# A reordered prologue with layer 0's input of the first sequence inside it, that sequence's buffers, and new places for the side pieces of the first and last turns

## What is computed

```python
# layer 0: two selective scans (one forward, one backward in time), 512 channels x 16 states
x_ssm = ln(x, norm1_g, norm1_b) * (1 + scale) + shift;  skip = x_ssm      # scale, shift, gate = silu(c) @ Wada.T + bada
x_ssm = ln(x_ssm, norm2_g, norm2_b)
mz = x_ssm @ Wz.T + bz;  act_mx = silu(x_ssm @ Wx.T + bx)
z1 = ssm(mz @ Wc1.T + bc1);  z2 = flip(ssm(flip(mz @ Wc2.T + bc2)))
x = x + gate * ((act_mx * z1 + act_mx * z2) @ Wf.T + bf + skip)
# layer 1: Mamba with a permutation of the tokens, a convolution of 4 taps and one selective scan
# layer 2: softmax attention, 16 heads;  layer 3: linear attention, 8 heads; both with a modulated norm and silu
# ssm(u): delta = softplus(..); h = exp(delta*A) * h + delta*B*u;  y = C . h, step by step over 256 tokens
```

## Time and profile before

| what | us |
|---|---|
| median of three runs | 3379.65 (3375.57 to 3383.61) |
| the profiled execution | 3382.8 |
| its span, first to last instruction | 3381.1 |
| TensorE, ScalarE, VectorE, GpSimd busy | 3058.3, 2878.3, 2690.2, 2666.1 |
| mean granted TensorE clock | 0.967 |

### The profile page before, as it was taken

The page is one execution under the profiler, slowest core; times in us unless marked ns, Lnnn a source line. Parts: engine busy times, 40 slices in busy tenths (PEclk is TensorE's granted clock), DMA queues, the critical chain, the costliest instruction groups (busy, mean ns, idle before and its releaser), DMA issues.

```text
span 3381.1 us, 63684 instructions
## 1 busy us (share of the span) xinstructions
PE 3058.3 (90%) x21758; PEld 2538.9 (75%) x21758; DVE 2690.2 (80%) x3435; ACT 2878.3 (85%) x6603; POOL 2666.1 (79%) x3086
## 2 busy tenths in 40 slices
PE   7577788999999999999999999999999999888876
PEld 3366677778788887888788888888887878777644
DVE  0377797979898998979898988989798978887632
ACT  1586889899999999999999999999999989887723
POOL 0296899889898898989898898989898978887600
PEclk8799999999999999999999999999999999999968
DMA  4122222222222222222222222222222222211100
GB/s 169 42 75 62 69 82 73 76 68 84 67 74 81 69 85 66 83 68 83 69 81 71 72 82 67 87 64 85 67 84 68 79 65 67 72 63 60 48 1 8
DMA packets 132289, 239.67 MB, mean 71 GB/s; under 512 B 15198, under 2 KB 30878, under 8 KB 131567
## 3 DMA queue, kind: packets, MB, share of 16 engines
q1 hardware_dynamic: 131968, 235.59, 22.6%
HBM read 230.45 MB, written 5.08 MB: 70 GB/s over the span
## 4 chain that ended last, share of the span: by engine, by line
PE 58%; ACT 16%; DVE 14%; issue 5%; POOL 4%; DMA 0%; DVEq 0%; ACTq 0%; SPq 0%; POOLq 0%
PE ps_b L959 13%; PE ps_y L987 12%; DVE hst L1067 8%; PE ps_v L1166 6%; ACT decay L1026 5%; PE ps_x L1690 3%; PE ps_x L1664 3%; PE ps_x L1172 3%; POOL g L1082 3%; ACT dbut L1037 3%; PE ps_x L1166 2%; PE ps_v L1172 2%; PE ps_v L1217 2%; PE ps_x L1700 2%; POOL dbut L1047 1%
## 5 line engine op out<-in xcount | busy, mean ns | idle before, releaser
L1082 POOL TENSOR_TENSOR g<-hst,c_bc 128x512 f32<-128x512 f32 x1536 | 1984.6, 1292 | 387.8 <-PE ps_y L987 320.2
L1067 DVE TENSOR_TENSOR_SCAN hst<-decay,ps_b 128x512 f32<-128x512 f32 x1536 | 1821.0, 1209 | 320.2 <-PE ps_b L959 157.1
L1026 ACT ACTIVATE decay<-delta,acoef 128x256 f32<-128x256 f32 x3072 | 1377.1, 497 | 18.0 <-DVE hst L1067 17.3
L959 PE MATMUL ps_b<-ident,dbut 128*128 128x128 f32 x6144 | 941.7, 276 | 144.1 <-DVE hst L1067 71.4
L987 PE MATMUL ps_y<-ident,g 128*128 128x128 f32 x6144 | 940.3, 276 | 16.5 <-ACT u L1378 14.6
L959 PEld LDWEIGHTS ps_b<-ident,dbut 128*128 128x128 f32 x6144 | 704.3, 142 | 222.0 <-issue 129.2
L1047 POOL TENSOR_SCALAR dbut<-dut,bcm 128x256 f32<-128x256 f32 x1536 | 759.2, 494 | 132.8 <-ACT dut L1277 132.8
L987 PEld LDWEIGHTS ps_y<-ident,g 128*128 128x128 f32 x6144 | 730.4, 142 | 141.8 <-issue 55.9
L1037 ACT ACTIVATE dbut<-dut,bcm 128x256 f32<-128x256 f32 x1536 | 765.8, 499 | 29.4 <-PE ps_b L959 27.2
L1773 DVE TENSOR_REDUCE mxt<-ps_x 128x4 f32<-128x1024 f32 x120 | 144.9, 1207 | 27.3 <-PE ps_x L1664 27.2
L1745 ACT ACTIVATE pT<-ps_x 128x1024 f32<-128x1024 f32 x120 | 121.5, 1012 | 43.4 <-PE ps_x L1700 39.2
(11 more groups left out here) (236 smaller groups left out, 3690.1 us busy)
## 6 DMA issues: line engine op xcount, KB each, us to landing
c_bc<-c_rows SPq DMA_DIRECT2D x768, 256.0 KB, 3.1
ada_w<-in_ada_w_dram SPq DMA_DIRECT2D x1, 5120.0 KB
weights<-in_weights_dram SPq DMA_DIRECT2D x1, 4320.0 KB, 33.8
x<-in_x_dram SPq DMA_DIRECT2D x16, 256.0 KB, 3.9
rows_bc<-mod_rows SPq DMA_DIRECT2D x16, 256.0 KB, 3.8
gate<-mod_rows SPq DMA_DIRECT2D x32, 128.0 KB, 3.6
out_dram<-x SPq DMA_DIRECT2D x16, 256.0 KB, 3.5
wc<-in_wc_dram SPq DMA_DIRECT2D x1, 2048.0 KB, 20.9
```

Source lines behind the costliest of these rows:

```text
L959: last = nc.tensor.matmul(ps_b[:, u % 2, e * T + t * P:e * T + (t + 1) * P], dbut[:, u % NDBU, t, e * P:(e + 1) * P], ident[:, :], is_tran ...
L1026: last = nc.scalar.activation(decay[:, u % (DA_AHEAD + 2), e, :], delta[slot(b, s)][:, eb, :], ACT.Exp, scale=acoef[:, s, eb, n:n + 1])
L1067: nc.vector.tensor_tensor_scan(line(hst[:, u % NHST, :, :].rearrange("p e t -> p (e t)")), line(decay[:, u % (DA_AHEAD + 2), :, :].rearran ...
L1082: nc.gpsimd.tensor_tensor(g[:, u % NG, :, :], hst[:, u % NHST, :, :], c_bc[:, k % NCB * CHUNK + n % CHUNK, :].unsqueeze(1) .broadcast_to([ ...
```

## The change

The prologue's block is moved behind the definitions of the pieces, since it now runs `l0_in` of sequence 0, interleaved by hand. Only the rows of layer 0 and the gates (4 D columns of modulation) are computed as rows; the six column groups are computed as columns, directly, from weights loaded into `u_s`, `delta` and others; zt comes from matmuls of wc and wz. The late weights are loaded when these columns are done, since `ada_b` stands in their place. `slot(0, 0)` is 2: scan 0 of sequence 0 uses the buffers of layer 1. The places of turns -1, 0, 1, 15, 16, 17 and 18 are new.

```diff
@@ places (SPECIAL), those the prediction speaks of
     -1: prep0
-            "PE": (46, 48, 49, 50, 56, 69, 72, 73),
+            "PE": (0, 0, 107, 107, 107, 107, 107, 107),
         prep1
-            "PE": (46, 48, 63, 64, 78, 88, 92, 96),
+            "PE": (107, 107, 111.25, 112, 117, 120, 122, 123),
         l0_mx
-            "PE": (85, 86, 90, 91, 96),
+            "PE": (107, 107, 111.5, 111.75, 114),
     0: prep0
-            "PE": (46, 48, 49, 50, 56, 69, 72, 73),
+            "PE": (36, 36, 38, 39, 42, 46, 47, 49),
         prep1
-            "PE": (46, 48, 63, 64, 78, 88, 92, 96),
-            "DVE": (78, 83, 86),
+            "PE": (62, 62.5, 63.5, 106.071, 106.357, 106.643, 106.857, 107),
+            "DVE": (106.2, 106.6, 106.8),
         l0_post
-            "PE": (43, 46, 74, 76, 79, 82, 82, 84),
+            "PE": (63, 64, 95, 96, 106.143, 106.214, 106.286, 106.429),
         l0_mx
-            "PE": (85, 86, 90, 91, 96),
+            "PE": (106.5, 106.571, 106.714, 106.786, 106.929),
     15: l1_post
-            "PE": (0, 4, 7, 7, 7, 7, 8, 9, 14),
+            "PE": (1.333, 2, 2.25, 2.333, 2.417, 2.667, 2.833, 2.917, 3.6),
         l2b
-            "PE": (5, 7, 10, 12, 15, 19, 19, 22, 22, 24, 25, 25, 28, 28, 30, 30, 32, 33, 34),
+            "PE": (1.667, 2.75, 3, 3.8, 4, 6, 6, 7.25, 8, 8.75, 9, 10, 14, 14, 17, 17, 19, 20, 21),
     16: l2a
-            "PE": (42, 43, 44, 44, 45, 45, 45, 45, 45, 45, 45, 45, 45, 45, 45, 45, 45),
+            "PE": (9, 12, 12, 12, 12, 14, 14, 16, 18, 20, 22, 24, 27, 30, 32, 35, 35),
         l2b
-            "PE": (-25, -23, -22, -20, -20, -18, -18, -13, -12, -6, -4, -3, 1, 1, 3, 3, 5, 7, 9),
+            "PE": (-43, -41, -41, -39, -39, -37, -37, -35, -35, -33, -33, -32, -29, -29, -27, -27, -25, -24, -22),
         l3
-            "PE": (19, 23, 23, 25, 25, 28, 28, 30, 32, 33, 36),
+            "PE": (-13, -10.375, -10.125, -9, -9, -7.667, -7, -4, -2, -1.333, 1),
     17: l2b
-            "PE": (5, 6, 7, 8, 8, 9, 10, 11, 12, 13, 14, 15, 16, 17, 17, 17, 17, 17, 17),
+            "PE": (-3, -2, 0, 5, 8, 10, 11, 13, 14, 16, 18, 19, 22, 23, 26, 27, 29, 31, 33),
@@ buffers and waits
         def slot(b, s):
+            if s == 0 and b == 0:
+                return 2
@@ prep_scalar
-            if s == 1:
+            if s == 1 and b >= 1:
+                after(act, b, "dt_full_0", 2)
+                after(act, b, "c_stored_0", 16)
+            if s == 2 and b == 0:
                 after(act, b, "dt_full_0", 2)
                 after(act, b, "c_stored_0", 16)
@@ l0_in_scalar
-                if b >= 1:
+                if b >= 1 and (b, k % 2) != (1, 0):
                     act.wait_ge(S["u_added"], scans.added[b - 1, k % 2, k // 2])
@@ prologue, SyncE
+                    for dst, src in ada: ...      # cond, ada_b, 4 D columns of ada_w (2.1 MB), norm_rows
+                    for dst, src in fold: ...     # wz, wc, columns
+                    for dst, src in rest: ...     # early weights, itok, wdt
+                    for dst, src in cols: ...     # the other 6 D columns of ada_w (3.1 MB)
+                    sp.wait_ge(S["rows_ready"], 2)
+                    sp.dma_start(mod_rows, rows[:, :, :].rearrange("b r d -> b (r d)")).then_inc(S["rows_stored"], 16)
...
+                    next(l0_load)
+                    next(l0_load)
+                    sp.wait_ge(S["cols_full"], 1)
+                    sp.dma_start(W[:, early:WTOT], dram["weights"][:, early:WTOT]).then_inc(stage_sems["weights_in"], 16)
@@ prologue, TensorE
+                    def zt_part(j):
+                        s_, half = j // 2, j % 2
+                        pt = bank((ps_x, ps_b)[s_], half, 2)
+                        for m in range(2):
+                            for k in range(EB):
+                                last = nc.tensor.matmul(pt[:, m, :], wc[:, s_, k, (2 * half + m) * P:(2 * half + m + 1) * P],
+                                                        wz[:, k, :], start=(k == 0), stop=(k == EB - 1))
+                    for j in range(2): ...        # two row blocks
+                        for k in range(EB):       # bias, 512 columns moving, for s_ = 0 and 1
+                            last = nc.tensor.matmul(row, c["bz"][:, k:k + 1], wc[:, s_, k, :], start=(k == 0),
+                                                    stop=(k == EB - 1))
...
+                    zt_part(ZT_ORDER[0])          # behind the fold
+                    zt_part(ZT_ORDER[1])
+                    next(l0)                      # the turn of sequence 0
...
+                    next(l0)
+                    next(l0)
+                    zt_part(ZT_ORDER[2])
+                    next(l0)
+                    next(l0)
+                    zt_part(ZT_ORDER[3])
+                    next(l0)
...
+                    for m in range(6 * DB):
+                        for k in range(CB_):
+                            part = ada_cols[k][:, m * P:(m + 1) * P] if m < 8 else ada_last[:, k, (m - 8) * P:(m - 7) * P]
+                            nc.tensor.matmul(ps_b[:, 0, m * B:(m + 1) * B], part, cond_s[:, k, :], start=(k == 0), stop=False)
+                        last = nc.tensor.matmul(ps_b[:, 0, m * B:(m + 1) * B], ada_b[:, 4 * D + m * P:4 * D + (m + 1) * P],
+                                                ones[0:1, 0:B], start=False, stop=True)
+                    last.then_inc(S["cols_full"], 1)
@@ main part
-                        if name in table and 0 <= i - back < LAST:
+                        if name in table and 0 <= i - back < LAST and (name, i) != ("l0_in", -1):
```

More of the change, by code:

```diff
@@ new lines, in build @@
+        S = stage_sems
+        bcm = [sb(f"bcm{s}", [P, TB, N]) for s in range(3)]
+        shared = sb("shared", [P, T])
+        dbc_a = shared[0:DBC, :]
+        dbc_b = sb("dbc_b", [DBC, T])
+        c_bc = sb("c_bc", [P, NCB * CHUNK, T])
+        decay = sb("decay", [P, DA_AHEAD + 2, HALF, T])
+        dbut = sb("dbut", [P, NDBU, TB, HALF * P])
+        hst = sb("hst", [P, NHST, HALF, T])
+        g = sb("g", [P, NG, HALF, T])
+        x1 = [sb(f"x1_{k}", [P, TB, D]) for k in range(2)]
+        x2 = [sb(f"x2_{k}", [P, TB, D]) for k in range(2)]
@@ new lines, in build @@
+        v3 = sb("v3", [P, TB, D])
+        xn_a = sb("xn_a", [P, TB, D])
+        xt_a = sb("xt_a", [P, DB, T])
+        xt_x = sb("xt_x", [P, DB, T])
+        gate1 = sb("gate1", [P, D])
+        act_x = sb("act_x", [P, EB, T])
+        act_z = sb("act_z", [P, EB, T])
+        yg = sb("yg", [P, EB, T])
+        xm = sb("xm", [P, EB, CT - 1 + T])
+        yt = sb("yt", [P, TB, E])
+        dbc = [dbc_b, dbc_b, dbc_a]
+        qT = sb("qT", [P, EB, T])
+        kT = sb("kT", [P, EB, T])
+        v2 = sb("v2", [P, TB, H2, DH2 + 1])
@@ new lines, in build @@
+        pT = sb("pT", [P, NPT, TB, T])
+        du = pT[:, :, :, :].rearrange("p a t n -> p (a t) n")
+        rec = sb("rec", [P, 2, TB, H2 // 2])
+        yv = sb("yv", [P, TB, D])
+        maskrow = sb("maskrow", [P, T])
+        usual = Attention(ps_x, (ps_x, 2), xt_x, qT, kT, v2, yv)
+        late = Attention(ps_b, (ps_v, B_), dbut[:, 0, :, :], decay[:, 0:2, :, :].rearrange("p a e t -> p (a e) t"),
+                         decay[:, 2:4, :, :].rearrange("p a e t -> p (a e) t"),
+                         dbut[:, 2:4, :, :].rearrange("p a t n -> p (a t n)")[:, 0:TB * H2 * (DH2 + 1)]
+                         .rearrange("p (t h l) -> p t h l", t=TB, h=H2), dbut[:, 1, :, :])
@@ L1962, in build @@
+        xt_l3 = sb("xt_l3", [P, DB, T])
+        xn_l3 = sb("xn_l3", [P, TB, D])
+        q3 = rows_bc[:, 0:TB, :]
+        k3 = xn_b
+        q3T, k3T = xt_l3, xn_l3
+        r3 = sb("r3", [P, 3, 16])
+        bd = shared[:, :].rearrange("p (d q) -> p d q", d=DB)
+        kmax = sb("kmax", [P, 4, DB])
         LAYER0, LAYER1 = ((0, 0), (1, 0), (0, 1), (1, 1)), ((2, 0), (2, 1))
@@ L2086, in lanes, with by_use @@
         return out
+    def by_use(m):
+        scale, shift = (4 * D, 6 * D, 8 * D), (3 * D, 7 * D, 9 * D)
+        return np.concatenate([m[..., 0:3 * D], m[..., 5 * D:6 * D]] + [m[..., o:o + D] for o in scale + shift], -1)
     one_row = np.zeros(P, np.float32)
```

811 lines of the change are left out of this document (397 added, 414 removed).

## The result

The changed kernel takes **3330.5 us** (median of 4 runs, 3327.3 to 3333.4) against 3378.2 for the kernel before in the same measurement: a ratio of 0.986, 95% interval 0.985 to 0.988. Forecast: 3307, range 3265 to 3350. The sign and the range hold; of the forecast gain of 73 us, 48 are there between the medians and 54 between the two profiled executions (3381.1 to 3326.9). One of the six executions of the last experiment took 5043.4 us at a granted clock of 0.557, against 0.98 in the other five, and is left out of its figures.

A forecast was written before the change was run, and what follows sets the result against it. Four full engines bound the long middle, GpSimd turn 0, so only the ends could gain: -26 - 10 - 37 = -73 us on the profiled 3382.8 gives 3310, as median 3307, range 3265 to 3350.

The forecast's parts named there:

- Term 1: Prologue up to the first scan: first scan at 120.5 instead of 146.29, -26 us (-18 to -33).
- the columns phase: Prologue, modulation columns as 120 records with 16 moving columns: 12.4 to 23.6 us, taken as 20.
- Term 2: Turns 0 and 1: separate buffers and new places shorten the wait between the turns, -10 us in sum.
- Gap: Between turns 0 and 1 (scans 63 and 64): the wait without scans shrinks from 28.3 to 6.5 us.
- knot: Tick 219, between scans 75 and 76 of turn 1: moved pieces stop the scans for 12 us, one scan covered.
- The rival with GpSimd's bound (-25): Turns 0 and 1 near GpSimd's bound, turns 15 and 16 at the middle's share: -103 us, 3277; chance 0.18.
- Term 3: The end: stages moved from behind the last scan into turns 15 and 16, +12 there and -49 behind, -37 us.
- The tail: Last scan to the end: only sequence 15's chain left, 148 us against 197, -49 (-32 to -56).
- The end packs badly: Rival: turns 15 and 16 take 309 us and the tail 165, -3 instead of -37, 3341; chance 0.20.
- Only exchanges waits: Rival: prologue swaps waits for TensorE work at half clock; projections, zt and columns add 8 to 15 us, 3318; chance 0.10.
- The late rows: Rival: prologue's row loads land 10 us later, sequence 0's input is not hidden, 3 us lost, 3310; chance 0.08.
- The slower rival: Stops of 12 to 14 us wherever a chain stands between two scans make the kernel slower, 3393; chance 0.04.

The follow-up runs named there:

- the last experiment: Changed kernel with modulation columns as rows and late silu, plus layer 0's input of sequence 1 some ten scans later and its preparation 0 eight: 3316.5 us.
- the old turns: Changed kernel with sequence 0 back in the buffers of layer 0 and turns 0 and 1 at the places of before: 3334.6 us, ratio 0.987.
- The ends alone: Kernel before the change with nothing but the new places of turns 15 to 18: 3350.5 us, ratio 0.991.

## Why the prediction was right in sign and 24 us short

**Term 1, -22 for -26: right, with one step mis-sized.** The queue of TensorE was walked correctly: the last projection of sequence 0 ended at 65.98 (forecast 66.1), though the weights came 1.8 us later than forecast (first matmul at 10.29) and dbcw took 3.8 where I had 6.0, because it now ran at full clock. That the first row block runs at half clock, as the forecast says, rests on its records alone (0.79 us each, 4.76/6, against 0.43 later); the profile prints a clock of 1.00 for that stretch in both kernels.

The step that was off is the columns phase, 25.2 for 20, and 27.3 to 27.7 in the five other kernels that have it; that is above the upper bound of 23.6. The fall of the clock came when the forecast needs it: at 75.7, 3.6 us into the phase, with TensorE busy without a gap, and with my prices for one-column records (0.103 and 0.197) the phase would have taken about 21. What was too low are the prices: records with 16 moving columns took 0.117 and 0.232. In the five others the clock fell 0.6 to 1.3 us into the phase, which is their 2 us.

The Trainium skill (TensorE: Matmul & The Clock Gate, LDWEIGHTS) prices a load by its columns, an estimated 12.8 us for the 120, so 0.107 a record. The trace has 9% more at full clock, and twice as much at half. The rule did point at the remedy: the form with rows loads 16 columns instead of 128 and took 14.7.

A further 1.9 us lie between the main part's start and the first scan (24.1 for 22.2). That the main part began only 2.1 us late is partly luck: dbcw, its bias and the barrier gave back 3.1 of the 5.2.

**Term 2, +3 for -10: the step that failed.** Gap (7.4 for 6.5) and knot (12.6 for 12) came as forecast, the knot with one wrong part. What failed is the sentence that the chain of preparation 1 "fits" in 11 scans of 1.72, at +1, and that everything else moved into turn 0 is free. I compared the length of a chain with the time of the scans; what counts is how much of it stands in one piece in a queue between two scans. GpSimd sets turn 0's pace, 1.70 us a scan, and cannot make up a stop. VectorE can: its scans come 1.1 to 1.2 us apart until it is some two scans ahead. So a block of 4 us is absorbed when nothing else stops VectorE for the next scans (the kernel before had one of 4.0 at scan 4 and one of 5.9 at scan 8, and lost 1.7 in all), and of blocks in quick succession the later ones find little of the lead left. GpSimd's product stands 3.7 us behind its scan once the pace has settled, which is that lead; it was 3.5 ahead of the block of 4.0 in the kernel before, and 2.0 ahead of the stop of 6.0 between scans 5 and 6 in the changed one.

That is why either of the two moved things alone costs nearly all of it: at scan 44 the changed kernel stands at 81.8, 81.3 with the preparation taken out, 81.9 with the input at its old places, and 76.5 with neither. The other 3.6 of the 8.9, up to scan 63, are one operation of preparation 0 of sequence 1 (the last rows of this document). The later input took back 4.8 us up to scan 32, as this account has it, and lost 3 at another place, which shows how little room there is; a rule by which the price of a given set of blocks could be foretold no run here gives.

The second failed step is scans 80 to 160, where I had put nothing for what was moved into turn 1 out of the gap: +5.0, and up to +8.2 in executions with the same places at a lower granted clock; the old turns give back 5.0. The gap was not idle time to be won. Its window in the kernel before (columns as above) holds 19.0 us of TensorE and 13.2 of ScalarE, and that work had to go where the scans are:

```profile
255.10:283.40 28.30, 19.02 (x90) 14.34 (x90) 11.01 (x17) 13.17 (x30) 5.38 (x7) 0.88 0.19 62
```

The rival with GpSimd's bound (-25) was wrong for the same reason. What came is near the other end (+5), by luck: that bound stood for a stop of 25 us in tick 219, which took 12.6.

**Term 3, -31 for -37: the mechanism right, one term mis-sized.** TensorE's work in turns 15 and 16 was forecast at 268 us and is 268; its share is 89%, not 92, so 300 and not 292. I had argued from VectorE's and ScalarE's room that the share would rise further; it rose from 87 to 89. What keeps it from the middle's 97% no run here tells. The ends alone, +24.6 there, say the same.

The tail gave 52.5 for 49; what left it is the stage l2a(14), 44.5 us behind the scans and 3.6 inside them. That move, with the places behind it that go with it, is worth some 40 us of the whole 48. Its mechanism was forecast: 33 us for sequence 14's stage ahead of sequence 15's, and 32 came back when it stood there again.

The mis-sized term is the cost in turns 15 and 16, +21 for +12. The earlier trace rows parts the two turns at 3122.4; turn 16's first scan before is at 3132.0. From scan to scan TensorE's work is this (turns 15 and 16 before, then changed; window, length, TensorE busy, clock, DMA share, GB/s):

```profile
2905.60:3132.00 226.40, 200.85 (x1464) 0.98 0.20 63
3132.00:3184.40 52.40, 41.30 (x320) 1.00 0.21 62
2882.60:3123.40 240.80, 214.20 (x1556) 0.97 0.19 59
3123.40:3182.70 59.30, 52.92 (x384) 1.00 0.20 64
```

Turn 15 got 13.3 us of work, took 14.4 longer and stayed at a share of 89%; turn 16 got 11.6, took 6.8 longer and rose from 79 to 89%. The room that the forecast counted on was found in turn 16 alone.

**The rivals.** "The end packs badly" (309 and 165) is out: 300 and 144. "Only exchanges waits" is right as to the clock of one phase, 75.7 to 97.3 at half, and wrong for the projections and zt, which ran at full. The late rows did not happen: the norm began at 34.4, where 37 to 38 was forecast. The slower rival needed six full knots. Only two stops of over 10 us came (12.6 and 10.7), and the tail gave 52 where it had 32. Its price for a knot is not refuted: scans 64 to 80 took 10.3 us more than before, about what the knot of tick 219 was charged. Its 3393 does not come out of the terms that it names; with the 22 us of the gap counted as won they give 3387.

**Not tried.** The knot at the start of turn 15 (10.7 us between scans 1413 and 1414, where l1_post(13), l1_in(14) and l2b(12) stand in three ticks) was taken apart in no run, so its share in the +14.4 of turn 15 is open.

## What to carry to other kernels

Before work is moved out of a gap, write down what each engine does in the gap: that work is added to the stretch it goes to, and there its price is set by the largest piece that stands between two steps of the pacing loop and by how soon the next such piece follows, not by the busy share. Before a long stop is spread, look for what else it hides: here a load that nobody had waited for became a stop of 8.9 us. Behind the last loop, where each step waits for the one before, a stage costs its whole chain (44.5 us here, with the places that go with it) and inside the loop it cost 3.6, so such stages are the ones to move first. And before two profiles are compared stage by stage, compare the granted clock of each stage: 3 us in a turn of 196 went with it.
